# A decoder layer with two attentions and routed experts: the order of POOL's and of PE's work inside a step of cross-attention

## The reference, cut to what matters

```
x = x + self_attention(layernorm(x))            # 16 heads of 8, a window of 32 keys, rotary
x = x + cross_attention(layernorm(x), ctx)      # 16 heads of 8, a window of 16 keys, biases
x = x + experts(layernorm(x))                   # 8 experts, the two best of each token
```

## Time and profile before

| | before |
|---|---|
| median of three runs | 567.29 us |
| span of the profiled execution | 562.7 us |
| steps 7 to 29 of cross-attention in it | 131.3 us (235.28 to 366.60 us) |
| PE busy in them | 125.75 us |
| DVE, ACT, POOL busy in them | 97.62, 107.50, 99.88 us |

### The profile page before, as it was taken

How to read it: one execution, slowest core, us unless ns; L and a number is a source line. 1 busy time by engine, 2 the same in 40 slices (tenths; PEclk the granted TensorE clock), 3 DMA queues, 4 the chain that set the end, 5 groups by cost and what they waited for, 6 DMA issues and landing times.

```text
span 562.7 us, 30637 instructions
## 1 busy us (share of the span) xinstructions
PE 485.7 (86%) x11903; PEld 400.6 (71%) x11903; DVE 372.7 (66%) x1314; ACT 332.5 (59%) x985; POOL 308.3 (55%) x413
## 2 busy tenths in 40 slices
PE   2689999999999798898999999973799999999930
PEld 2367777777776566676777777751599999999920
DVE  5467888888877355677877777665166666666626
ACT  3367778777786576787888887852134343343400
POOL 2444455445536343577778786767055555555624
PEclk9999999999999898999999999985799999999985
DMA  8211111111110000011111111012222222222139
GB/s 234 77 57 50 47 57 56 48 50 51 56 58 23 13 17 13 23 48 31 38 33 38 33 41 37 28 36 85 48 68 72 67 64 71 65 67 72 48 138 322
DMA packets 40801, 34.93 MB, mean 62 GB/s; under 512 B 6413, under 2 KB 37263, under 8 KB 40736
## 3 DMA queue, kind: packets, MB, share of 16 engines
q1 hardware_dynamic: 24752, 19.62, 11.1%
q0 software_dynamic: 4320, 8.53, 4.6%
q10 hardware_dynamic: 11664, 5.88, 4.4%
HBM read 18.58 MB, written 11.68 MB: 54 GB/s over the span
## 4 chain that ended last, share of the span: by engine, by line
PE 79%; issue 6%; DVE 4%; DMA 3%; SPq 2%; POOL 2%; ACT 1%; ACTq 1%; DVEq 0%; POOLq 0%
PE p_scores L1029 11%; PE p_probsT L533 11%; PE p_att_bank L523 8%; PE p_scores L416 8%; PE p_att_bank L1038 6%; PE p_v_bank L1038 5%; PE p_scores L461 4%; PE p_v_bank L486 4%; PE p_scores L409 4%; PE p_att_bank L471 3%; PE p_qk L437 2%; PE p_qk L428 2%; PE p_v_bank L502 2%; PE p_att_bank L820 2%; SPq L330 2%
## 5 line engine op out<-in xcount | busy, mean ns | idle before, releaser
L662 POOL TENSOR_TENSOR k_heads<-qk,consts 128x512 f32<-128x512 f32 x64 | 66.8, 1044 | 99.8 <-DVE qk L724 58.2
L1114 POOL DMA_INDIRECT expert_results<-weighted,result_at x71 | 75.5, 1063 | 71.5 <-DVE weighted L1102 49.1
L737 DVE TENSOR_REDUCE shift<-p_scores 128x8 bf16<-128x512 f32 (+1 forms) x128 | 74.1, 619 | 24.0 <-PE p_scores L416 23.5
L1078 ACT ACTIVATE hidden<-p_scores 128x512 f32<-128x512 f32 x71 | 42.4, 597 | 78.9 <-PE p_scores L1029 58.7
L560 ACT COPY probsT<-p_probsT 128x512 f32<-128x512 f32 x128 | 75.6, 590 | 21.1 <-PE p_probsT L533 21.0
L533 PE MATMUL p_probsT<-consts,probs 128*128 128x128 f32 x512 | 80.0, 280 | 0.4
L566 ACT ACTIVATE probs<-p_scores 128x512 f32<-128x512 f32 x128 | 78.0, 610 | 0.3 <-PE p_scores L461 0.3
L1029 PE MATMUL p_scores<-gotT,w_now 128*128 128x128 f32 x568 | 76.7, 279 | 1.6 <-ACT gotT L1081 1.6
L878 POOL DMA_INDIRECT sent_rows<-row,slot_u x64 | 64.3, 1005 | 15.8 <-issue 15.8
L1029 PEld LDWEIGHTS p_scores<-gotT,w_now 128*128 128x128 f32 x568 | 70.5, 195 | 1.8 <-ACT gotT L1081 1.8
L619 ACT COPY values<-p_v_bank 32x128 f32<-32x128 f32 x256 | 68.4, 267 | 2.2
(11 more groups left out here) (133 smaller groups left out, 951.6 us busy)
## 6 DMA issues: line engine op xcount, KB each, us to landing
got<-sent_rows ACTq DMA_DIRECT2D x71, 66.0 KB, 1.9
swapped<-raw SPq DMA_DIRECT2D x64, 64.0 KB, 1.9
w<-w_in SPq DMA_DIRECT2D x32, 128.0 KB, 2.3
back<-expert_results SPq DMA_DIRECT2D x8, 512.0 KB, 6.6
ctxT<-ctxT_in SPq DMA_DIRECT2D x32, 64.0 KB, 1.9
out<-x SPq DMA_DIRECT2D x8, 256.0 KB, 5.2
x<-x_in SPq DMA_DIRECT2D x4, 448.0 KB, 9.8
expert_results<-weighted,result_at POOLq DMA_INDIRECT x71, 2.4
```

The lines of the kernel that those rows point to most:

```text
L662: nc.gpsimd.tensor_tensor(k_heads[:, :, BLK:], qk[:, 1:2, :].to_broadcast([P, G, P]), cv(C_HEAD, G).unsqueeze(2).to_broadcast([P, G, P]), ...
L737: nc.vector.tensor_reduce(shift[:, half * 8:half * 8 + 8], p_scores[:, half * 8:half * 8 + 8, low:WIN], AX.X, ALU.max).then_inc(s_max, 1)
L1114: nc.gpsimd.indirect_dma_start(out=results, out_offset=bass.IndirectOffsetOnAxis(ap=result_at[:, slot:slot + 1], axis=0), in_=weighted[:, ...
```

## The change

Two things move, in cross-attention only. On PE the function `turn_rows` (the transposes L495 and L502 of before) now stands in front of V's 16 matmuls instead of behind them. On POOL the two indirect DMAs stand at the end of the step, behind the deviation, instead of behind `k_heads`; the tile they send is c-5 instead of c-6. So the rows of a given tile are sent just before the next step's `k_heads` instead of just after it. The table `LAST_SENDS` is adapted so that the last ten DMAs still follow the last deviation.

```diff
-        LAST_SENDS = {B - 1: [B - 6], B: [B - 5], B + 1: [B - 4, B - 3], B + 3: [B - 2, B - 1]}
+        LAST_SENDS = {B + 1: [B - 4, B - 3], B + 2: [], B + 3: [B - 2, B - 1], B + 4: [], B + 5: []}
...
+                if not own:
+                    if runs(h, c, 3) or runs(h, c, 2) or runs(h, c, -2):
+                        v_bank_read()
+                    turn_rows(h, c)
                 if runs(h, c, 2):
-
-                    v_bank_read()
+                    if own:
+                        v_bank_read()
                     src = xnT[:, (c + 2) % 2, :] if own else ctxT[:, (c + 2) % 2, :]
...
-                if not own and runs(h, c, -2):
-
-                    n = at(-2)
-                    if not runs(h, c, 2):
-                        v_bank_read()
-                    nc.tensor.wait_ge(s_xn3, n + 1)
-                    nc.tensor.transpose(p_x3T, xn3[:, (c - 2) % 4, :], ident).then_inc(s_x3Traw, 1)
-                if runs(h, c, 3 + ahead):
-
-                    n = count(3 + ahead)
-                    if not runs(h, c, 2):
+                if own:
+                    if runs(h, c, 3 + ahead) and not runs(h, c, 2):
                         v_bank_read()
-                    nc.tensor.wait_ge(s_xn, n + 1)
-                    nc.tensor.transpose(p_xT, xn[:, (c + 3 + ahead) % 2, :], ident).then_inc(s_xTraw, 1)
+                    turn_rows(h, c)
...
+            def turn_rows(h, c):
+                if not own and runs(h, c, -2):
+
+                    nc.tensor.wait_ge(s_xn3, TURN * h + (c - 2) + 1)
+                    nc.tensor.transpose(p_x3T, xn3[:, (c - 2) % 4, :], ident).then_inc(s_x3Traw, 1)
+                if runs(h, c, 3 + ahead):
+
+                    nc.tensor.wait_ge(s_xn, TURN * h + (c + 3 + ahead + base) + 1)
+                    nc.tensor.transpose(p_xT, xn[:, (c + 3 + ahead) % 2, :], ident).then_inc(s_xTraw, 1)
...
-                if not own and (not isinstance(h, int) or c < B):
-                    route_pool(h, c, [c - 6])
                 yield
...
-                if not own and isinstance(h, int) and c in LAST_SENDS:
-
-                    route_pool(h, c, LAST_SENDS[c])
+                if not own:
+                    route_pool(h, c, LAST_SENDS.get(c, [c - 5]) if isinstance(h, int) else [c - 5])
```

## The result

The changed kernel takes 577.91 us (median of 5 runs, 577.44 to 581.88), the kernel before in the same session 567.24 us (5 runs, 562.49 to 568.52). The ratio is 1.0196 with an interval of 1.0156 to 1.0235: slower by some 11 us (567.24 x 0.0196). Forecast were 576.0 us and a span longer by 8.7 us.

A forecast was written before the change was run, and what follows sets the result against it. PE was taken to set the pace, 5.71 us per step, with DVE's loop of 5.44 just under. Held DVE instructions +9.2 us, steps -3 to 6 -0.5: +8.7 on 567.3 gives 576.0 us, range 566 to 580.5.

The forecast's parts named there:

- PE's part: Last transpose of the probabilities to the values' first matmul: 0.91 us instead of 1.07, 0.16 us less per step.
- The 3.64 us from the statistics to `k_heads`: POOL, cross-attention: from the end of DVE's statistics over deviation and two DMAs to the start of `k_heads`, 3.64 us.
- `k_heads` 0.68 us behind the addition: POOL's `k_heads` would lie from 0.68 to 1.72 us behind DVE's addition, over DVE's routing work.
- the 2.96 us from the statistics to the next addition: DVE, each step: the next addition comes 5.44 - 2.48 = 2.96 us after the statistics.
- Which instruction is held, and how long: DVE routing held by `k_heads`: L940 in odd steps, delay 0.74 to 1.05 us; cast L917 in even, 0.29 to 0.5.
- DVE's loop through PE: Cross-attention step: 5.44 us before; with the mean delay of 0.52 to 0.78 added, 5.96 to 6.22 us.
- POOL's chain: Statistics over deviation, DMAs and `k_heads` to the masks: allows steps of no less than 5.38 us, costs nothing by itself.
- Where PE waits: PE idle before the shift matmuls on DVE's maxima, some 0.4 us per step; wrong if the wait sits at the masks.
- Rival A: DVE's small instructions are not held: about -1 us in the 23 steps, -0.5 before, 565.8 us; chance 0.18.
- B: PE's gain is whole because the DMAs end sooner than added up: -4.2 us, 563.1 us; chance 0.06.
- C: DVE's instructions held only in part, mean delay 0.25 us: +3.5 less 0.5, 570.3 us; chance 0.18.
- `xn` keeping GpSimd from its descriptors: By the skill's rule the DMAs beside DVE's `xn` could take some 0.6 us more; the forecast added nothing.

The follow-up runs named there:

- e10: The changed kernel with DVE's 1 + ratio done as a tensor_reduce over a pair instead of a tensor_scalar: 575.34 us, ratio 1.0163.
- e2: The kernel before with only the POOL part of the change (DMAs at the end of the step), PE's order as before: 578.03 us, ratio 1.0199.
- e6: The kernel before with one of POOL's two DMAs in front of `k_heads` and the other behind it: 577.47 us, ratio 1.0235.
- e3: The changed kernel with DVE's routing work behind its statistics, except the part that frees the PSUM bank: 559.86 us, ratio 0.9864; repeated 560.41 us, 0.9894.
- e9: The kernel before with DVE's routing work behind its statistics, nothing else: 566.01 us, ratio 0.9982.

## Why the prediction was right, point by point

- **PE's part**: -0.16 us per step, -3.7 in 23 steps, by one change of form. Right in the trace (V to values 0.24 to 0.33 us instead of 0.76, one pause instead of two). Alone it brought 2.1 us (0.9962) instead of up to 4.2; that it would vanish in the whole change was right (577.91 with it, 578.03 without).
- **The 3.64 us from the statistics to `k_heads`**: right, 3.69 (320.17 - 316.48).
- **`k_heads` 0.68 us behind the addition**: too early. It came 1.06 and 1.20 us behind (320.17 - 319.11, 314.24 - 313.04). The term that failed is the 2.96 us from the statistics to the next addition, which measured 2.63 (316.48 to 319.11): it held PE's work of before, 1.48 us from the wait for the maxima on. From the end of the maxima to the addition it is now 1.23 us (317.88 to 319.11) instead of 1.65 (316.67 to 318.32).
- **Which instruction is held, and how long**: the mechanism was right, the sizes were not. Even steps: the cast took 0.94 us (0.71 in the mean) where 0.4 was forecast, the delay of the statistics was 0.72 in the median instead of 0.29 to 0.5, since `k_heads` lay later. Odd steps: not L940's counterpart (L941) with 0.9 but mostly L933 with 1.66, a delay of 1.45 instead of 0.74 to 1.05. The sentence that failed is "the DMAs' own instructions are not of this kind: the routing work runs at 0.17 beside the DMAs". It was read from instructions that started early in a DMA or had a pause of POOL behind it, and it does not carry over to the DMA with `k_heads` behind it (rows in the last section). There L933 took 0.16 us only in the two steps in which it started 0.30 us into the DMA (at 357.25 and 369.43), and 1.65 where it started 0.41 us into it; in those two steps the product L941, 0.79 us into the DMA, was held instead, 1.27 us. The kind was drawn too wide as well: "a DVE instruction with its operands in SBUF" takes in reduces, reciprocals and statistics, and these went through (0.15 us for the reduce of `e10`).
- **Both errors met a third, the loop**: the forecast put the delay on top of DVE's loop through PE, 5.44 + 0.52 to 0.78 us, and said of POOL's chain that by itself it costs nothing. The delay was 1.1 us in the mean of odd and even, but the loop is another, from the statistics over the DMAs and `k_heads` to the held instruction and back, without PE, and the time from the statistics to the next addition shrank by 0.3 to 0.4 us. Its 6.25 us happen to lie just above the forecast's 5.96 to 6.22. So the stretch grew by 12.2 us (at 0.96 of the clock; by 10.0 in `e2` at 1.00) where 5.8 to 11.8 stood. The total was near by luck in part, not because each size was right.
- **Where PE waits**: forecast was the maxima, 0.4 us per step, and "wrong if the wait sits at the masks". Most of the listed wait does sit at the masks (11.9 us, 17 times). I had set the masks as a sign that POOL's chain decides instead of the hold. They do not tell the two apart: POOL's chain is half of the loop, and PE waits for DVE once more behind the masks. The sign was badly chosen; the hold stands as a cause (`e6`, `e10`), together with the chain.
- **Rival A (nothing is held)** fell by the rows of L933 and L918, **B** by the time itself and by `e2`, **C** (held in part, 570.3) by `e2`.
- **The Trainium skill** (SBUF — State Buffer, Who interferes with whom) on `xn` keeping GpSimd from its descriptors: the DMA beside `xn` took 1.06 us (317.83, `xn` at 317.79), as elsewhere, so no 0.6 us came from there. What the page says in the other direction, that the engine that comes second blocks whole, is near to what this case paid for, with the exception of L933's order of coming above.
- **The tail and the experts**: unchanged, 196.13 against 196.10 us, as forecast.

## What to carry to other kernels

When an instruction of POOL is moved, ask first what DVE runs beside its new place, by kind: products from PSUM, statistics, maxima, reduces and reciprocals went through, while copies, casts, `tensor_scalar` and products of two SBUF operands, however small, were held to the end of POOL's product, and where a DMA stood right in front of the product, from 0.32 us into the DMA on. Where such work must lie beside POOL, order DVE so that the kinds that go through, here the statistics that the loop needs, stand there: the POOL order that cost 2.0% then brought 0.5 to 0.8%, and the changed kernel with it 1.1 to 1.4% (`e3`, faster than both kernels). And read the lengths of small instructions as well as the list of waits: a DVE instruction on two columns that takes 1.65 us is a wait for POOL, and ties the two engines into a loop that no wait in the list shows.

## What the runs showed of the hardware that was not expected

Beside an indirect DMA of POOL, too, DVE's small instructions were held, but what decided was the POOL instruction behind the DMA. In before, L932 starts 0.42 us into a DMA, as L933 does in the changed kernel, and takes 0.16 us; POOL pauses behind that DMA:

```profile
318.41 1.06 POOL L878 DMA_INDIRECT sent_rows<-row,slot_u  x1 [0.17 <-issue]
318.83 0.16 DVE L932 TENSOR_SCALAR ratio<-ratio 128x2 f32<-128x2 f32 x1
319.77 0.96 POOL L878 DMA_INDIRECT sent_rows<-row,slot_u  x1 [0.30 <-issue]
```

I counted the routing's copies, casts, `tensor_scalar` and products of two SBUF operands over all fourteen traces, from 230 to 390 us. Of those that started 0.32 to 0.50 us into a DMA, all 59 were held where `k_heads` (or its memsets) or the bias addition stood at most 0.04 us behind the DMA. None of 44 was held where POOL paused for 0.18 us or more behind it (41) or the deviation's instruction on two columns followed (3). Up to 0.31 us into a DMA all but one went through, whatever followed. Later in a DMA with a pause behind it, 0.51 to 0.80 us, 10 of 68 were held to its end, for 0.28 to 0.37 us.

How far they were held differs: with `k_heads` or its memsets behind the DMA, to the end of these (1.55 to 1.71 us in all for the `tensor_scalar`); with the bias addition behind it, only to about the DMA's own end (the copy at 313.02 in `e9` ends at 313.55, the DMA at 313.58). Between `k_heads` and the bias addition, which follows it as closely, the held ones did get in: the cast of step 313.04 ends at 315.32, the bias addition at 315.70. Memsets of POOL, which read nothing, held a `tensor_scalar` and a cast as its products did. What makes the difference between 0.31 and 0.32 us into the DMA, and between the two kinds of follower, was not tried.
